# A four-layer graph network on one core: matmuls of ones on TensorE, an earlier table load on ScalarE, and a new order on ScalarE in the last unit

## What is computed

```python
def _layernorm(x, axis=-1, eps=1e-05):
    m = jnp.mean(x, axis=axis, keepdims=True)
    v = jnp.var(x, axis=axis, keepdims=True)
    return (x - m) / jnp.sqrt(v + eps)

# layer 0
h = (1.0 + eps) * x + einsum('bnf,bnm->bmf', x, adj)
y = maximum(h @ W1 + b1, 0.0) @ W2 + b2                   # times the node mask
# layer 1
out = relu(concat([x, einsum('bid,bij->bjd', x, adj) / adj.sum(-1)[:, :, None]]) @ W.T + b)
# layer 2
out = einsum('bnm,bmo->bno', normalized(adj + I), x @ weight) + bias
# layer 3, only for pairs (i, j) that adj joins
h = relu((x @ W1[:H])[:, :, None, :] + (x @ W1[H:])[:, None, :, :] + b1)
y = layernorm(h @ W2 + b2) * gamma + beta
out = einsum('bij,bijh->bih', adj, y)
```

## Time and profile before

| what | us |
|---|---|
| median of 3 runs | 462.51 |
| lowest and highest | 462.26 and 462.81 |
| the profiled execution, device time | 461.34 |
| its span on the core (first to last instruction) | 459.6 |
| around the span | 1.74 |
| busy: PE, DVE, ACT, POOL | 436.0, 414.5, 386.6, 354.1 |

### The profile page before, as it was taken

The page is one execution under the profiler, slowest core; times in us unless marked ns, Lnnn a source line. Parts: engine busy times, 40 slices in busy tenths (PEclk is TensorE's granted clock), DMA queues, the critical chain, the costliest instruction groups (busy, mean ns, idle before and its releaser), DMA issues. The chain is left out here.

```text
span 459.6 us, 14156 instructions
## 1 busy us (share of the span) xinstructions
PE 436.0 (95%) x3427; PEld 413.2 (90%) x3427; DVE 414.5 (90%) x1523; ACT 386.6 (84%) x1003; POOL 354.1 (77%) x651
## 2 busy tenths in 40 slices
PE   3799989999999999999999999999999999999991
PEld 3699989999999999889998999999999999999991
DVE  5799999999999999996998898889889988988966
ACT  2378979999999899998798888888888888888973
POOL 5289979999999899745777687778777776868652
PEclk9999999999999999999999999999999999999996
DMA  6133345445445652233323131322222222313011
GB/s 221 41 105 111 93 151 161 156 137 182 148 148 164 213 190 89 65 116 113 122 70 99 53 102 52 88 66 76 78 70 84 65 89 62 92 51 98 24 49 48
DMA packets 50939, 47.60 MB, mean 104 GB/s; under 512 B 5584, under 2 KB 42576, under 8 KB 50896
## 3 DMA queue, kind: packets, MB, share of 16 engines
q1 hardware_dynamic: 49328, 46.16, 32.7%
q10 hardware_dynamic: 1568, 0.96, 0.7%
HBM read 28.22 MB, written 18.87 MB: 102 GB/s over the span
## 5 line engine op out<-in xcount | busy, mean ns | idle before, releaser
L1575 PEld LDWEIGHTS bank<-w2c,hE 128*128 128x128 f32 x512 | 67.3, 192 | 2.4
L1575 PE MATMUL bank<-w2c,hE 128*128 128x128 f32 x512 | 67.5, 275 | 0.0
L905 ACT ACTIVATE hE<-bank,front 128x512 f32<-128x512 f32 x64 | 44.3, 691 | 7.6 <-PE bank L1556 7.4
L925 ACT ACTIVATE sqE<-bank 128x512 f32<-128x512 f32 x63 | 37.7, 599 | 12.9 <-PE bank L1575 12.5
L1230 DVE TENSOR_REDUCE ssum<-sqE 128x4 f32<-128x512 f32 x63 | 42.7, 677 | 4.4 <-ACT sqE L925 2.9
L1097 DVE BATCH_NORM_STATS2 stats<-t 128x6 f32<-128x128 f32 x192 | 44.5, 273 | 1.5 <-issue 1.4
L703 POOL TENSOR_TENSOR gHl<-gH,gHu 128x512 fp32r<-128x512 f32 x32 | 41.1, 1285 | 5.7 <-ACT gHu L879 5.7
L1255 DVE TENSOR_TENSOR ym<-bank,wE 128x512 f32<-128x512 f32 x64 | 43.2, 682 | 1.6 <-POOL wE L752 0.3
L719 POOL TENSOR_TENSOR half<-ym 128x512 f32<-128x512 f32 x31 | 39.4, 1273 | 3.3 <-DVE ym L1255 3.1
L1606 PE MATMUL bank<-yC,ST 128*128 128x128 f32 x256 | 34.3, 277 | 3.1 <-ACT yC L944 3.1
L1573 PE MATMUL bank<-bias,ones_b 128*128 128x512 bf16 x96 | 36.5, 380 | 0.6 <-DVE ym L1255 0.6
(11 more groups left out here) (189 smaller groups left out, 1628.5 us busy)
## 6 DMA issues: line engine op xcount, KB each, us to landing
hh_scratch<-hh SPq DMA_DIRECT2D x32, 256.0 KB, 2.2
gH<-hh_scratch SPq DMA_DIRECT2D x32, 256.0 KB, 2.8
A<-adj_groups SPq DMA_DIRECT2D x32, 128.0 KB, 2.1
res_scratch<-res SPq DMA_DIRECT2D x32, 128.0 KB, 2.0
gRES<-res_scratch SPq DMA_DIRECT2D x32, 128.0 KB, 2.4
AT<-adjT_groups SPq DMA_DIRECT2D x30, 128.0 KB, 2.3
out<-y SPq DMA_DIRECT2D x30, 128.0 KB, 1.9
X<-x_groups SPq DMA_DIRECT2D x28, 128.0 KB, 2.2
```

The costliest lines, as they stand in the source:

```text
L905: nc.scalar.activation(hE[g][:, :], HE_ps, ACT.Relu, bias=C["L3_b1"]).then_inc(b[f"hE{g}_ready"], 1)
L925: nc.scalar.activation(sqE[g][:, :, :], YE_ps[g], ACT.Square).then_inc(b[f"sqE{g}_ready"], 1)
L1575: last = nc.tensor.matmul(ps[:, i, :], hidden[:, i * P:(i + 1) * P], w2c[:, :], start=False, stop=i == tiles - 1)
```

## The change

PE gets a helper `keep_busy(bk, times)`. Each time it multiplies the tile of ones by itself, 512 columns wide, into a whole bank that nothing else uses at that moment; nobody reads the result. It is called nine times over ahead of PE's first work (bank 7), behind `hidden0` and `mlp0a` of groups 0 and 1 in the first round (2 and 1 matmuls), and eleven times over ahead of the scatter of unit 31 (bank 0). DVE sets `ones_b` first of all, and PE's first nine matmuls wait for this alone. The table load moves ahead of four of ACT's loads, and AT of 2, X of 3 and the diagonal are issued by SP instead of ACT. In the last unit, ACT takes the root of unit 29 ahead of the squares, and makes y of unit 28 between esd and yC.

```diff
-        last_ready = sem("last_ready")
+        last_ready, s_ones = sem("last_ready"), sem("ones_set")
@@ sync
             load(A[3][:, :, :], a_d, 3, a_loaded[3])
+            load(AT[2][:, :, :], at_d, 2, at_loaded[2])
+            load(X[3][:, :, :], x_d, 3, x_loaded[3])
             load(AT[3][:, :, :], at_d, 3, at_loaded[3])
+            sp.dma_start(diag[:, :], diag_d).then_inc(s_diag, 16)
@@ scalar
             load(X[1], x_d, 1, x_loaded[1])
+            nc.scalar.preload_act_table(ACT.Sqrt)
             act.dma_start(mask8[:, :], mask_d).then_inc(s_mask, 16)
             load(AT[1], at_d, 1, at_loaded[1])
             load(X[2], x_d, 2, x_loaded[2])
-            load(AT[2], at_d, 2, at_loaded[2])
-            load(X[3], x_d, 3, x_loaded[3])
-            act.dma_start(diag[:, :], diag_d).then_inc(s_diag, 16)
-            nc.scalar.preload_act_table(ACT.Sqrt)
@@ square_ell
                 def stage(q, u, count):
+                    if at_end(u) and g == 1:
+                        out_std(q, u - 2, lambda d=0: count(d + 2))
                     act.wait_ge(b[f"YE{g}_psum"], count())
@@ spread
                 if at_end(u):
+                    apply_out(1 - q, u - 3, lambda d=0: count(d + 3))
                     act.wait_ge(b["wE_ready"], count())
@@
+            def middle_std(q, u, count):
+                if not (isinstance(u, int) and u == UNITS - 3):
+                    out_std(q, u, count)
+
             def middle_apply(q, u, count):
-                if not (isinstance(u, int) and u in (UNITS - 3, UNITS - 1)):
+                if not (isinstance(u, int) and (u >= UNITS - 4) and u != UNITS - 2):
                     apply_out(q, u, count)
@@
-                      ("sqc", square_csr), ("std", spread), ("fstd", out_std), ("app", middle_apply)]
+                      ("sqc", square_csr), ("std", spread), ("fstd", middle_std), ("app", middle_apply)]
@@ vector
+            nc.vector.memset(ones_b[:, :], 1.0).then_inc(s_ones, 1)
             nc.vector.memset(bias0[:, :, :], 0.0)
-            nc.vector.memset(ones_b[:, :], 1.0)
@@ tensor
+            def keep_busy(bk, times):
+
+                for _ in range(times):
+                    nc.tensor.matmul(run(spans(bk)), ones_b[:, :], ones_b[:, :].unsqueeze(1).to_broadcast([P, 4, P]), start=True, stop=True)
+
+            pe.wait_ge(s_ones, 1)
+            keep_busy(bank[7], 9)
             pe.wait_ge(s_setp, 2)
@@ hidden0, and the same behind the matmul of mlp0a
+                if isinstance(r, int) and r == 0 and k < 2:
+                    keep_busy(bank[7], 2 - k)
@@ scatter
+                if at_end(u):
+                    keep_busy(bank[0], 11)
                 pe.wait_ge(b["yC_ready"], count())
```

## The result

The changed kernel takes **459.65 us** (median of 5 runs, 458.92 to 460.91); the kernel before took 462.26 in the runs beside it (461.69 to 462.81). The ratio is 0.9949 with an interval of [0.9929, 0.9969]: faster by 2.6 us, where 4.4 were forecast. The same kernel was timed twice more, on two chips, at 458.70 (ratio 0.9917 [0.9898, 0.9935]) and 459.48 (0.9942 [0.9929, 0.9955]). Over all 16 runs its median is 459.4. So the forecast of 458.1 was right in direction and too good by 1.3 us (all 16 runs) to 1.55 (the first five), and the range 457.0 to 460.6 holds the result. As a gain over before, the miss is 1.8 us in the first timing and 0.6 and 1.7 in the two others.

A forecast was written before the change was run, and what follows sets the result against it. PE was taken to bound 24 to 446 us (418.6 of 422 busy), so only start and end could gain. 462.51 less 4.4 (3.3 at the start, 1.1 at the end) gave 458.1, bounds 457.2 to 459.3, wider range 457.0 to 460.6.

The forecast's parts named there:

- The end: Last unit: earlier root, wE and accE no longer behind POOL, scatter kept fast; 1.1 us gained, bounds 0.4 and 1.3.
- the eleven ones: Matmuls ahead of the last scatter keep it at 1.06 us instead of 1.54, protecting 0.15 to 0.2 us.
- The table load: ACT's start: issued earlier, the load ends near 3.5 us, giving 0.45 us on the path of group 0.
- loads held: Rival: the table load delays AT of 1 by 2.66 us; start gives 1.8 us, whole 459.6; chance 0.07.
- The ones at the start: PE's nine fillers, 0.44 us each, end near 5.1 at no cost; clock rises during hidden0 of group 0.
- Clock late: Rival: fillers don't raise the clock before group 1's products; start gives about 1.0 us, time 460.4; chance 0.13.
- fillers in full: Rival: each filler costs 0.64 us and the clock stays low until about 16 us; time 465.2, chance 0.04.
- sum0 of group 1: DVE's residual of group 1 starts at 12.45 to 12.7 us instead of 15.88, 3.2 to 3.4 us earlier.
- Start given back: Rival: DVE or PE later meets a wait hidden by its lateness, only the end's gain remains; 461.4, chance 0.06.
- A pipeline that is full 3 us earlier hands over those 3 us whole: Start to finish: the start's lead stays undiminished, as orders are fixed and later loads move along.
- the sign of being wrong: A DVE or PE wait between 15 and 60 us that was not there before would show the forecast wrong.
- The term of the start: Pipeline fill: 3.3 us gained, taken from the earlier residual of group 1 on DVE; bounds 2.8 and 4.0.

The follow-up runs named there:

- order_only: The kernel before with only the new order of ACT in the last unit, no matmuls of ones: 461.06 us, ratio 0.9983.
- fill_only: The kernel before with only the matmuls of ones at the start: 460.52 us, ratio 0.9971.
- after_b: The changed kernel once more, unaltered, as yardstick on another chip: 459.48 us, ratio 0.9942 to the kernel before.
- hold_b: The changed kernel plus sixteen more matmuls of ones in PE's waits of the first round, second timing: 458.53 us, ratio 0.9909 to the kernel before.
- start_only: The changed kernel without its two edits of the end (ACT's order, eleven matmuls of ones): 460.19 us, ratio 0.9959 to the kernel before.
- again: The changed kernel once more under a new name, as yardstick on its chip: 458.70 us, ratio 0.9917 to the kernel before.

## Why the prediction was right, and where it was too good

**The end: right.** 1.1 us was forecast and 1.13 measured, in every kernel that has the order, and all three steps are seen: the root of unit 29 ahead of the squares, wE free of POOL, tout out of accE's way. One term of it was wrong: the eleven ones were given 0.15 to 0.2 us, and order_only has the same 1.1 in its profile without them. The sum had carried the 1.54 us of the scatter over to a scatter that starts after 2.52 us of idle time instead of 3.09.

**The table load: right in the mechanism.** The load of 1.28 us ends at 3.51 and holds no transfer, so "loads held" is out. Alone it gave 0.26 us of sum0 (0.45 was forecast for group 0) and no time; beside the ones it may have given more, as the one execution of fill_only suggests.

**The ones at the start: right on PE.** They cost about 0.45 us each, ended at 5.15 (5.1 forecast), and the level was up from mlp0a on. PE's result of group 0 was there at 9.99 (9.8 to 10.05 forecast). "Clock late" and "fillers in full" are out.

**sum0 of group 1: 0.1 to 0.8 us too late.** It came at 13.48, 12.79 and 13.14 in the three profiles of after, instead of 12.45 to 12.7. The failing step is "DVE needs 13.75 + 0.60 − 11.70 = 2.65 us from there to the end of its normalization". These durations had been read where POOL was idle: in before its steps for groups 2 and 3 were over at 12.98, ahead of x at 13.75. In after x starts at 12.45, these steps last until 15.03, and x takes 1.10 instead of 0.60. In after_b sum0 of group 0 starts at 10.04 and that of group 1 3.10 us later. In after the late mask took another 0.4.

**"Start given back": too small a chance, and half true.** The sentence that failed is "A pipeline that is full 3 us earlier hands over those 3 us whole". It held from r4 on, within half a us: 405.1 to 406.1 us to the total of unit 29 in all kernels, against 405.51 before. (0.33 us of the weak gain of the profiled execution went there, 405.84 in after, and no run explains it.) It failed between sum0 of group 1 and r4, where before takes 20.11 us and the three profiles of after 22.88, 22.47 and 21.58. So of the leads of 2.40, 3.09 and 2.74 us, 2.77, 2.36 and 1.47 were given back. I named DVE or PE meeting a wait that their lateness had hidden as the form of this rival, and took it as all or nothing with 0.06. What came was PE's wait for DVE's one-time work, 0.99 us instead of none, 1.91 instead of 1.41 and 1.02 instead of 0.61, and with it a second fall of the clock (0.1 to 2.1 us, and 1.0 between the two heaps of executions). That DVE would wait for PE behind this, 1.29 us at 27.34, is the sign of being wrong that I had named. With the clock held, hold_b still takes 21.13 us over this way, 1.02 more than before: 0.57 is the x of group 1, and 0.44 comes behind r1, where DVE never waits but a later x takes 1.32 us instead of 0.94. These durations beside POOL differ between executions anyway, so how much of them the earlier start brings stays open. The sum used the clock only up to 17 us and at the end, and took the granted 1.00 in between as given.

**The sum.** The start is worth 1.9 us by start_only (ratio 0.9959, interval 1.2 to 2.6 us) instead of 3.3, and the end 1.2. These 1.4 us are as large as the miss of the time. The term of the start was mis-sized; its lower bound of 2.8 was a bound on sum0 alone and left the way behind it out, and two of the three leads at sum0 (2.40 and 2.74) lie under it too.

Of the kernels timed, hold_b is the fastest by its ratio, 0.9909 [0.9893, 0.9925], and beats both before and after on its chip.

## What to carry to other kernels

A lead at one step is not a lead at the end: follow it through the waits that stand behind it, and ask of each wait of the critical engine how much longer it gets. When a step moves to another time, read anew what its neighbours do at that time, because its duration may have been read beside an idle one. If matmuls of ones are used to raise the clock at the start, look for the next place where TensorE waits and fill it as well, and check afterwards with the granted clock by stretches that each filler protects something.

## What the hardware showed that I had not expected

The time at the lower level near 20 to 28 us was either about 3.4 or about 6.8 us in the eight profiles that have it, also for one and the same program (6.8, 6.8 and 3.4 in after, again and after_b).

The first loads land more than 1 us apart between executions, whatever their order: the cast of the mask starts between 7.67 and 9.28 us, and at 9.14, 7.97 and 7.81 in three profiles of one program. In before DVE's wait for PE would hide this; in after it put sum0 off by 0.4 us. The spread is over half of the effect under study, and before alone spans 460.8 to 463.5 us over its runs.

Who of DVE and POOL stands behind the other can't be read from the starts, which agree to 0.02 us. x of group 1 took 1.01 us in three profiles (before, order_only, start_only) and 1.58 in eleven, with the same order on both engines.
